# Twelve row buffers, two and four turns between slot stages, and part of the late work behind the slots: an RWKV layer with a routed expert layer

## The chip, the cores and the metric

One core of one Trainium2 chip. The metric is the device time of one execution in microseconds. The profile is of one execution on the same core; its times are counted from the start of its span.

## What is computed

`x` has 16 x 512 = 8192 tokens of 128 float32 features. Two parts are applied one after the other:

```python
x = x + _L0_attn_ref(_layernorm(x), ...)   # RWKV time mix (a scan over 512 steps) and channel mix
x = x + _L0_ffn_ref(_layernorm(x), ...)    # shared expert + one routed expert of 16

logits = hidden @ router_w.T
top_vals, top_idx = jax.lax.top_k(logits, 1)
scores = sigmoid(top_vals) at top_idx, 0 elsewhere
gate, up = split(einsum('nth,nhf->ntf', hidden * scores, gate_up_proj), 2)
expert_sum = einsum('ntf,nfh->nth', up * silu(gate), down_proj).sum(0)
shared = silu(hidden @ shared_gate_w.T) * (hidden @ shared_up_w.T) @ shared_down_w.T
```

Each token goes to a single expert of width 128. The shared expert has width 512 and is applied to all tokens.

## The kernel before, in words

**Rounds.** The tokens are 16 tiles of 512. In 23 rounds (`one_round`, one list per engine) the tiles go through a software pipeline: layer norms, time mix, channel mix, router, and the shared expert. At the end of a tile its rows, the scaled and normed features (128 columns), the token's number (1 column) and the base, that is everything but the routed expert (128 columns), are scattered to a table in DRAM, `sorted_rows`, grouped by expert: four indirect DMAs of GpSimd for each tile. The table is filled up with rows that name no token (`filler`).

**Late halves.** The shared expert is done per half tile of 256 tokens. Twelve halves (`LATE`, line 52) aren't finished before their tile is scattered. Their shares are computed later, kept in SBUF (`sh_of`) and added to `out` at the very end. Three of the twelve (u = 0, 1, 2) are done in the rounds, nine (u = 3 to 11) after them. One of these nine has four steps: step 0 and 1 are a gate and an up product each (`unit_product`, line 394, eight matmul pieces), with the activation on ScalarE (line 695) and the product on VectorE (line 1066); steps 2 and 3 are the two halves of the down product (`unit_down_late`, line 402, eight pieces each), after which ScalarE copies the share out of PSUM (line 698). `late_order` (line 238) lists the 36 steps. The first runs in the rounds, four more ahead of the turns (`STEPS_BEFORE` = 5, line 642), and 31 are spread over the turns by `late_steps` (line 250).

**Slots and turns.** A slot is 128 sorted rows of one expert. There are 80 slots, 40 pairs. The last is always empty: 8192 rows and 16 experts can need at most 79. A pair k goes through these steps:

- SP loads it from `sorted_rows` into a row buffer, two DMAs of 128.5 KB (line 370), after the store of the pair that used the buffer before. There are `RING` = 8 buffers. Ahead of pair 8 (`FILL_PAIR`) SP also issues 16 filler DMAs (line 362).
- TensorE transposes the features of two pairs at a time (line 651), VectorE copies them out of PSUM (line 1075).
- ScalarE copies the two experts' weights (line 814).
- TensorE makes gate and up (lines 658 and 659), ScalarE applies the activation (line 819), VectorE multiplies (line 1083).
- TensorE makes the down product (line 665), VectorE adds it to the base in the row buffer (line 1078).
- GpSimd stores the pair to `out` by token number, two indirect DMAs (line 1215); rows that name no token are left out.

Each engine runs a list of turns m. In turn m come the transposes of pairs m and m+1 (m even), gate and up of pair m - `GU_BEHIND`, the down product, add and store of pair m - `DN_BEHIND`, then the late steps of the turn. `GU_BEHIND` = 1 and `DN_BEHIND` = 2, so there are 42 turns.

**The end.** `add_late` (line 302): SP and ACT wait for the last stores of all row buffers, load six half tiles of `out` each (128 KB), VectorE adds the late shares (line 1093) once all are there, and SP and ACT store them again.

Of the kernel before, what the change touches and what calls it, by code (L numbers as in the profile page):

```python
# [28 lines left out]
P = 128  # L29
# [4 lines left out]
T = S  # L34
# [9 lines left out]
NP = NS // 2  # L44
RING = 8
PACK = 5
# [4 lines left out]
A_TILES, B_TILES, C_TILES = (0, 1, 2, 3, 4, 5, 6, 7, 8, 9, 10, 11, 12, 13, 14), (2, 5, 8, 11, 14), (13, 14, 15)  # L51
LATE = [(0, 1), (1, 1), (3, 1), (4, 1), (6, 1), (7, 1), (9, 1), (10, 1), (12, 1), (13, 1), (15, 1), (15, 0)]
N_LATE = len(LATE)

# [38 lines left out]
def program(nc, x, w_main, w_exp, vecs, out):  # L93
# [4 lines left out]
    with ExitStack() as ctx:  # L98
# [124 lines left out]
        FULL_SLOTS = NTOK // P - NE  # L223
        FILL_PAIR = 8
        FIRST_LATE = len(C_TILES)
        STEPS_BEFORE, LATE_TURN = 5, 1
        GU_BEHIND, DN_BEHIND = 1, 2
        W_BEHIND = GU_BEHIND - 1
# [21 lines left out]
        def late_steps(m):  # L250

            steps = late_order()[STEPS_BEFORE:]
            return [step for i, step in enumerate(steps) if LATE_TURN + i * (NP - 2) // len(steps) == m]

# [14 lines left out]
        def laps(i):  # L269

            return len(range(i, NP, RING))

# [5 lines left out]
        def stored(k):  # L278

            i, lap = k % RING, k // RING + 1  # L280
            if i < 8:
                return f"xout{i}", 32 * lap
            if i == 11:
                return "xout11", 32 * lap
            return f"scat{i - 8}", 16 * G * len(range(i - 8, NT, 3)) + 32 * lap

# [6 lines left out]
        def tl_of(u):  # L293
            return shared[:, u * HALF:(u + 1) * HALF]

        def tl_sem(u):

            if u < 8:
                return f"xr_in{u}", 32 * laps(u)
            return f"x_in{u - 8}", 16 * (NT // XR) + (32 * laps(u) if u < RING else 0)  # L300

        def add_late(eng, units):


            for k in range(NP - RING, NP):
                eng.wait_ge(s[stored(k)[0]], stored(k)[1])
            def place_of(u):
                tile, half = LATE[u]
                row = tile * T + half * HALF
                return out[row:row + HALF, :].rearrange("(p g) d -> p (g d)", g=2)  # L310
            for u in units:
                eng.dma_start(tl_of(u), place_of(u)).then_inc(s[tl_sem(u)[0]], 16)
            for u in units:
                eng.wait_ge(s["tl_add"], u + 1)
                eng.dma_start(place_of(u), tl_of(u)).then_inc(s["tl_out"], 16)
            eng.wait_ge(s["tl_out"], 16 * N_LATE)
# [10 lines left out]
        def _(sp):  # L327
# [30 lines left out]
            for k in range(NP):  # L358
# [10 lines left out]
                for j in range(2):  # L369
                    sp.dma_start(xr[k % RING][:, j, :], sorted_ap[bass.ds(first_rows[at_ + j], P), :]).then_inc(  # L370
                        s[loaded(k)[0]], 16)
            add_late(sp, range(0, N_LATE, 2))


        @block.tensor
        def _(pe):
# [69 lines left out]
            def one_round(n):  # L446
# [8 lines left out]
                for t in at(3):  # L455
                    wait(pe, "xn2T", t)
                    if t == 0:
                        pe.wait_ge(s["w_in1"], 16)
                    wait(pe, "hsg0", t - 2)
                    wait(pe, "sg0", t - 2)  # L460
# [24 lines left out]
                for t in at(3):  # L485
                    wait(pe, "xn2T", t)
                    wait(pe, "hac0", t - 2)
                    wait(pe, "ac0", t - 2)
# [121 lines left out]
                for t in at(3):  # L610
                    wait(pe, "k20", t)
                    wait(pe, "base", t - 2)
                    wait(pe, "hbase", t - 2)
                    wait(pe, "cbase", t - 2)
                    wait(pe, "rv", t - 1)
# [59 lines left out]
        def _(act_e):  # L675
# [147 lines left out]
            for m in range(TURNS):  # L823
                one_turn(m)
            add_late(act_e, range(1, N_LATE, 2))


        @block.vector
        def _(dve):
# [259 lines left out]
            for u in range(N_LATE):  # L1089
                dve.wait_ge(s[tl_sem(u)[0]], tl_sem(u)[1] + 16)  # L1090
                wait(dve, "cbase", NT)
                wait(dve, "lsh", N_LATE)
                v.tensor_tensor(tl_of(u), tl_of(u), sh_of(u), ALU.add).then_inc(s["tl_add"], 1)
# [3 lines left out]
        def _(gp):  # L1097
# [113 lines left out]
            def one_turn(m):  # L1211
                for k in pair(m, DN_BEHIND):
                    wait(gp, "xy", k)
                    for j in range(2):
                        g_.indirect_dma_start(  # L1215
# [43 lines left out]
```

## Time and profile before

| | us |
|---|---|
| median of 3 runs | 559.82 (559.63 to 560.57) |
| profiled execution, its time | 561.58 |
| profiled execution, span from the first to the last instruction | 559.9 |
| mean granted TensorE clock | 0.97 of full |
| busy: TensorE, VectorE, ScalarE, GpSimd | 490.7, 400.1, 322.9, 348.1 |

The busy times are sums over the whole span. The rounds end at about 400 us, and the turns fill the time from there to about 541. A matmul of float32 is recorded in several pieces that overlap, 275 ns each for 128 columns, and its end is modelled.

### The profile page before, as it was taken

Reading aid. Unit: us, or ns where it says so; the run is one execution under the profiler, and the core shown is the slowest. Engines: PE = TensorE matmul, PEld = TensorE weight load, DVE = VectorE, ACT = ScalarE, POOL = GpSimd, SP = SyncE. Lnnn points to the kernel's source line nnn. Section 1 sums busy time; section 2 is a strip of 40 time slices with the busy share of each in tenths; the row PEclk is TensorE's granted clock in tenths of the full one; section 3 lists DMA queues with packets and bytes.
Section 4 is the critical chain, followed back from the end, with each engine's and each line's share of the span. In section 5 each row is a group of like instructions: output and inputs, shape, how many; then the busy total and the mean of one; then the engine's idle time right before and its main releaser. Section 6 shows DMA issues by size and latency. Waiting matters only on the chain.

```text
span 559.9 us, 10321 instructions
## 1 busy us (share of the span) xinstructions
PE 490.7 (88%) x3012; PEld 399.6 (71%) x3012; DVE 400.1 (71%) x1098; ACT 322.9 (58%) x579; POOL 348.1 (62%) x542
## 2 busy tenths in 40 slices
PE   1778999999999999999999999999897879796930
PEld 0336778878778788687777787799796778786830
DVE  3678899998999899997999978745534343333323
ACT  3766977867867678767678664432344353444410
POOL 5364668867887688785878745636245556464660
PEclk9888999999999999999999999999999999898975
DMA  6003201101011011010110000111486344333207
GB/s 207 1 1 145 119 2 58 32 27 55 5 56 58 2 58 38 21 58 2 56 58 10 30 21 20 38 39 39 140 204 172 116 113 119 109 108 93 77 4 226
DMA packets 32424, 38.26 MB, mean 68 GB/s; under 512 B 4946, under 2 KB 28634, under 8 KB 32113
## 3 DMA queue, kind: packets, MB, share of 16 engines
q1 hardware_dynamic: 25008, 23.40, 14.5%
q0 software_dynamic: 5632, 12.63, 6.5%
q10 hardware_dynamic: 1728, 1.57, 0.9%
q8 instruction: 25, 0.41, 0.3%
q14 instruction: 31, 0.25, 0.1%
HBM read 21.15 MB, written 17.47 MB: 69 GB/s over the span
## 4 chain that ended last, share of the span: by engine, by line
PE 60%; DVE 10%; issue 9%; ACT 7%; another core or an unknown queue 6%; POOL 5%; DMA 1%; ACTq 0%; POOLq 0%; SPq 0%; DVEq 0%
PE bank L394 12%; PE bank L387 7%; PE bank L411 5%; PE bank L381 3%; PE bank L402 3%; PE bank L659 3%; PE bank L462 2%; PE bank L479 2%; DVE an L871 2%; PE bank L502 2%; PE bank L658 2%; PE bank L515 2%; PE bank L466 2%; PE bank L490 2%
## 5 line engine op out<-in xcount | busy, mean ns | idle before, releaser
L1215 POOL DMA_INDIRECT out<-shared x80 | 78.8, 985 | 71.3 <-DVE shared L1078 48.8
L394 PE MATMUL bank<-hT,wm 128*128 128x256 f32 x512 | 122.0, 382 | 0.9 <-ACT er L722 0.7
L394 PEld LDWEIGHTS bank<-hT,wm 128*128 128x128 f32 x512 | 94.0, 191 | 18.2 <-issue 7.5
L387 PE MATMUL bank<-wm,k 128*128 128x128 f32 x512 | 63.9, 280 | 2.8 <-ACT k L726 2.8
L387 PEld LDWEIGHTS bank<-wm,k 128*128 128x128 f32 x512 | 62.4, 196 | 4.4 <-ACT k L726 3.6
L1078 DVE TENSOR_TENSOR shared<-bank,shared 128x256 f32<-128x256 f32 x40 | 17.0, 424 | 42.0 <-PE bank L665 22.8
L871 DVE TENSOR_SCALAR an<-a,mvC,smC 128x128 f32<-128x128 f32 x64 | 43.2, 735 | 1.4 <-POOL smC L1125 1.4
L819 ACT ACTIVATE er<-bank 128x256 f32<-128x256 f32 x40 | 15.3, 384 | 48.9 <-remote 22.8
L411 PEld LDWEIGHTS bank<-wm,actA 128*128 128x128 f32 x240 | 30.2, 192 | 6.7 <-issue 6.7
L1204 POOL TENSOR_SCALAR shared<-shared,smA 128x128 f32<-128x128 f32 x64 | 34.6, 549 | 0.3
L411 PE MATMUL bank<-wm,actA 128*128 128x128 f32 x240 | 31.6, 275 | 0.0
L742 ACT ACTIVATE xn1tok<-shared,smA 128x128 f32<-128x128 f32 x64 | 26.2, 479 | 7.1 <-POOL smA L1161 7.1
L1199 POOL TENSOR_TENSOR q<-num,q 128x128 f32<-128x128 f32 x16 | 7.3, 454 | 32.4 <-DVE q L1015 32.4
L1159 POOL TENSOR_TENSOR smA<-smA,half 128x8 f32<-128x8 f32 x16 | 26.4, 1648 | 1.3
L1169 POOL DMA_INDIRECT sorted_rows<-rows,posi x16 | 21.3, 1334 | 9.3 <-DVE posi L934 3.6
L871 DVE TENSOR_SCALAR h<-rows,mvE,smE 128x128 f32<-128x128 f32 x64 | 23.7, 436 | 3.8 <-POOL smE L1125 3.6
L1188 POOL DMA_INDIRECT sorted_rows<-rows,posi x16 | 22.6, 1416 | 4.9 <-issue 4.9
L766 ACT ACTIVATE kr<-bank 128x512 f32<-128x512 f32 x16 | 9.6, 597 | 26.6 <-PE bank L462 26.6
L381 PE MATMUL bank<-ident,xn1tok 128*128 128x128 f32 x64 | 10.1, 283 | 14.6 <-ACT xn1tok L742 14.6
L1141 POOL TENSOR_SCALAR rows<-h,sc 128x128 f32<-128x128 f32 x64 | 22.7, 365 | 0.3
L1174 POOL TENSOR_TENSOR xa<-shared,a 128x512 f32<-128x512 f32 x16 | 21.1, 1316 | 0.5
L930 DVE TENSOR_TENSOR ew<-bank,ew 128x512 f32<-128x512 f32 x16 | 10.9, 683 | 14.6 <-PE bank L515 9.6
(240 smaller groups left out, 1357.6 us busy)
## 6 DMA issues: line engine op xcount, KB each, us to landing
shared<-sorted_rows SPq DMA_DIRECT2D x80, 128.5 KB
shared<-x SPq DMA_DIRECT2D x16, 256.0 KB
wexp<-w_exp SPq DMA_DIRECT2D x2, 1536.0 KB, 8.4
sorted_rows<-filler SPq DMA_DIRECT2D x17, 128.5 KB
out<-shared POOLq DMA_INDIRECT x80
sorted_rows<-rows,posi POOLq DMA_INDIRECT x64
wm<-w_main SPq DMA_DIRECT2D x1, 776.0 KB, 8.1
shared<-out SPq DMA_DIRECT2D x6, 128.0 KB
```

The source lines that it names most:

```text
L381: ins = nc.tensor.transpose(grp(dst, g), grp(src, g), ident[:, :])
L387: ins = mm(grp(acc, g), grp(lhs, g), W(name, f), start=(f == 0 and g == 0), stop=(f == F // P - 1), skip_group_check=True)
L394: ins = mm(dst[:, j * HALF:(j + 1) * HALF], W(name, 2 * pair_ + j), src[:, half * HALF:(half + 1) * HALF], start=True, stop=True)
L411: ins = mm(grp(acc, 2 * half + g), lhs[:, at_:at_ + P], W("down", 2 * pair_ + j), start=(pair_ == 0 and j == 0 and g == 0), stop=(pair_ == ...
L742: ins = af(grp(xn1tok[t % 2], g), grp(xin[t % XR], g), ACT.Identity, bias=smA[t % 3][:, 5, g:g + 1], scale=smA[t % 3][:, 4, g:g + 1])
L871: ins = v.tensor_scalar(grp(dst, g), src(g), mv[:, g, 0:1], rs[:, g:g + 1], ALU.subtract, ALU.mult)
L1141: ins = g_.tensor_scalar(rows[t % 3][:, g, 0:D], grp(h[t % 2], g), sc[t % 2][:, g:g + 1], 1.0, ALU.mult, ALU.mult)
L1159: g_.tensor_tensor(sm[:, 3:5, :], sm[:, 1:3, :], half8[:, :, :], ALU.pow).then_inc(s["pA"], 1)
L1169: g_.indirect_dma_start(sorted_ap, bass.IndirectOffsetOnAxis(posi[t % 3][:, 1:2].bitcast(U32), 0), rows[t % 3][:, 1, :], None).then_inc(s[ ...
L1188: g_.indirect_dma_start(sorted_ap, bass.IndirectOffsetOnAxis(posi[t % 3][:, 0:1].bitcast(U32), 0), rows[t % 3][:, 0, :], None).then_inc(s[ ...
L1204: ins = g_.tensor_scalar(grp(xn0[t % 4], g), grp(xin[t % XR], g), smA[t % 3][:, 0, g:g + 1], smA[t % 3][:, 3, g:g + 1], ALU.add, ALU.mult)
L1215: g_.indirect_dma_start(out, bass.IndirectOffsetOnAxis(xr[k % RING][:, j, D:D + 1].bitcast(U32), 0), xr[k % RING][:, j, D + 1:ROW], None, ...
```

## The change

Seven things are changed:

1. `RING` is 12. Buffers 8 to 11 are the three tiles of rows that the rounds use for the scatter.
2. `GU_BEHIND` is 2 and `DN_BEHIND` 4; the weight copy is one turn later too. There are 44 turns.
3. `STEPS_BEFORE` is 3. The two steps that so remain ((3, 2) and (4, 1)) run in turns 0 and 1, the next 19 spread over turns 4 to 39, and the last 12 in turns 40 to 43, one each in 40, 41 and 42 and nine in 43, behind the turn's own work.
4. The filler DMAs are issued ahead of pair 12.
5. The second slot of the last pair isn't stored, and the waits for that store count 16 less.
6. At the end SP alone waits for the stores and loads the late halves, two halves with one DMA; ACT only stores. VectorE adds half u once its own share is there, not all.
7. The last two late halves change places, and three pairs of waits of TensorE in the rounds change their order.

```diff
-RING = 8
+RING = 12
-LATE = [(0, 1), ..., (13, 1), (15, 1), (15, 0)]
+LATE = [(0, 1), ..., (13, 1), (15, 0), (15, 1)]
...
-        FILL_PAIR = 8
+        FILL_PAIR = 12
-        STEPS_BEFORE, LATE_TURN = 5, 1
-        GU_BEHIND, DN_BEHIND = 1, 2
+        STEPS_BEFORE, LATE_TURN, LATE_AFTER = 3, 4, 12
+        GU_BEHIND, DN_BEHIND = 2, 4
...
             steps = late_order()[STEPS_BEFORE:]
-            return [step for i, step in enumerate(steps) if LATE_TURN + i * (NP - 2) // len(steps) == m]
+            if m < 2:
+                return steps[m:m + 1]
+            if m >= NP:
+                last, at_ = steps[len(steps) - LATE_AFTER:], m - NP
+                return last[at_:at_ + 1] if m < TURNS - 1 else last[at_:]
+            between = steps[2:len(steps) - LATE_AFTER]
+            return [step for i, step in enumerate(between) if LATE_TURN + i * (NP - LATE_TURN) // len(between) == m]
...
-            i, lap = k % RING, k // RING + 1
+            i, lap, none = k % RING, k // RING + 1, 16 if k == NP - 1 else 0
...
+        def stores(k):
+            return range(2) if k < NP - 1 else range(1)
...
-        def add_late(eng, units):
+        def all_stored(eng):
             for k in range(NP - RING, NP):
                 eng.wait_ge(s[stored(k)[0]], stored(k)[1])
...
-            for u in units:
-                eng.dma_start(tl_of(u), place_of(u)).then_inc(s[tl_sem(u)[0]], 16)
+        def load_late(eng):
+            halves_ = out.rearrange("(h p g) d -> p h (g d)", p=P, g=2)
+            for u in range(0, N_LATE, 2):
+                a0, a1 = first_row(u) // HALF, first_row(u + 1) // HALF
+                eng.dma_start(shared[:, u * HALF:(u + 2) * HALF].rearrange("p (h c) -> p h c", h=2),
+                              halves_[:, a0:a1 + 1:a1 - a0, :]).then_inc(s[tl_sem(u)[0]], 16)
...
-            add_late(sp, range(0, N_LATE, 2))
+            all_stored(sp)
+            load_late(sp)
+            store_late(sp, range(0, N_LATE, 2))
...
-            add_late(act_e, range(1, N_LATE, 2))
+            store_late(act_e, range(1, N_LATE, 2))
...
             for u in range(N_LATE):
-                dve.wait_ge(s[tl_sem(u)[0]], tl_sem(u)[1] + 16)
+                if u % 2 == 0:
+                    dve.wait_ge(s[tl_sem(u)[0]], tl_sem(u)[1] + 16)
                 wait(dve, "cbase", NT)
-                wait(dve, "lsh", N_LATE)
+                wait(dve, "lsh", u)
...
-                    for j in range(2):
+                    for j in stores(k):
                         g_.indirect_dma_start(
```

## Rows read from the trace of the kernel before

**Rows 1.** Timeline, 541 to 560 us: start, us, engine, line, operation, count [idle before, releaser]
```profile
541.27 0.42 DVE L1078 TENSOR_TENSOR shared<-bank,shared 128x256 f32<-128x256 f32 x1 [0.80 <-PE bank L665]
...
544.42 0.98 POOL L1215 DMA_INDIRECT out<-shared  x1 [0.30 <-issue]
545.71 0.98 POOL L1215 DMA_INDIRECT out<-shared  x1 [0.30 <-issue]
547.89 2.71 SPq L312 DMA_DIRECT2D shared<-out  x6
...
550.26 1.59 DVE L1093 TENSOR_TENSOR shared<-shared,xn1tok 128x256 f32<-128x256 f32 x4 [8.57 <-DMA shared<-out]
...
554.77 1.43 DVE L1093 TENSOR_TENSOR shared<-shared,ew 128x256 f32<-128x256 f32 x4
```

**Rows 2.** Busy by stretch: us, each engine's busy (count), TensorE clock, DMA share, GB/s
```profile
404.00:541.30 137.30, 112.90 (x811) 105.17 (x809) 52.68 (x115) 58.69 (x144) 74.59 (x76) 0.96 0.43 117
480.00:490.00 10.00, 10.00 (x70) 9.79 (x69) 3.92 (x9) 3.75 (x10) 5.86 (x6) 0.83 0.37 113
490.00:500.00 10.00, 9.56 (x73) 8.94 (x72) 4.39 (x9) 5.29 (x14) 5.60 (x7) 1.00 0.32 94
500.00:510.00 10.00, 5.56 (x38) 5.19 (x37) 2.70 (x6) 2.90 (x7) 4.91 (x6) 0.92 0.48 138
```

**Rows 3.** Waits of 404 to 541.3 us: in total, times, longest
```profile
POOL out L1215 <- DVE shared L1078: 48.8, 15, 14.4
...
ACT er L819 <- remote: 22.8, 8, 4.0
...
DVE shared L1078 <- remote: 16.4, 8, 3.8
...
PE bank L658 <- DVE num L1075: 9.0, 3, 4.4
...
PE bank L665 <- DVE e L1083: 6.7, 8, 2.2
...
PE bank L658 <- ACT th L814: 4.0, 1, 4.0
```

**Rows 4.** Timeline, 452 to 460 us
```profile
452.28 1.10 PE L402 MATMUL bank<-wm,den 128*128 128x128 f32 x8
...
453.22 0.60 PE L651 MATMUL bank<-ident,shared 128*128 128x128 f32 x4
...
455.00 1.89 PE L394 MATMUL bank<-hT,wm 128*128 128x256 f32 x8
...
457.67 0.38 ACT L698 ACTIVATE xn1T<-bank 128x256 f32<-128x256 f32 x1 [5.25 <-remote]
457.73 0.69 DVE L1075 COPY er<-bank 128x512 f32<-128x512 f32 x1 [4.33 <-remote]
...
459.02 0.46 PE L658 MATMUL bank<-er,an 128*128 128x128 f32 x2 [2.13 <-ACT an L814]
```

**Rows 5.** The page's part 4, by engine, over the whole span
```profile
PE 60%; DVE 10%; issue 9%; ACT 7%; another core or an unknown queue 6%; POOL 5%; DMA 1%; ACTq 0%; POOLq 0%; SPq 0%; DVEq 0%
```

**Rows 6.** The chain that ended last, in order of time: start, us, what
```profile
439.35 0.44 PE bank L651 x4
...
440.45 0.22 PE bank L659 x2
440.68 0.45 PE bank L665 x4
441.12 1.73 PE bank L394 x8
...
444.19 0.94 PE bank L402 x8
```

**Rows 7.** Timeline, 400 to 411 us
```profile
402.55 1.89 PE L394 MATMUL bank<-hT,wm 128*128 128x256 f32 x8
```

**Rows 8.** Timeline of SP's queue, 396 to 426 us
```profile
398.74 9.01 SPq L370 DMA_DIRECT2D shared<-sorted_rows  x16
408.96 9.70 SPq L362 DMA_DIRECT2D sorted_rows<-filler  x16
420.09 5.24 SPq L370 DMA_DIRECT2D shared<-sorted_rows  x6
```

**Rows 9.** Line 1215: ns of one min/median/max, first and last start
```profile
L1215 POOL DMA_INDIRECT out<-shared x80: 982/984/1005, 411.0 to 545.7; - x80
```

**Rows 10.** DMA issues of 544 to 560 us: KB, us to landing
```profile
out<-shared SPq DMA_DIRECT2D x6, 128.0 KB, 3.2
```

More of the change, by code:

```diff
@@ L51 @@
 A_TILES, B_TILES, C_TILES = (0, 1, 2, 3, 4, 5, 6, 7, 8, 9, 10, 11, 12, 13, 14), (2, 5, 8, 11, 14), (13, 14, 15)
-LATE = [(0, 1), (1, 1), (3, 1), (4, 1), (6, 1), (7, 1), (9, 1), (10, 1), (12, 1), (13, 1), (15, 1), (15, 0)]
+LATE = [(0, 1), (1, 1), (3, 1), (4, 1), (6, 1), (7, 1), (9, 1), (10, 1), (12, 1), (13, 1), (15, 0), (15, 1)]
 N_LATE = len(LATE)
@@ L278, in stored @@
         def stored(k):
-            i, lap = k % RING, k // RING + 1
+            i, lap, none = k % RING, k // RING + 1, 16 if k == NP - 1 else 0
             if i < 8:
-                return f"xout{i}", 32 * lap
+                return f"xout{i}", 32 * lap - none
             if i == 11:
-                return "xout11", 32 * lap
-            return f"scat{i - 8}", 16 * G * len(range(i - 8, NT, 3)) + 32 * lap
+                return "xout11", 32 * lap - none
+            return f"scat{i - 8}", 16 * G * len(range(i - 8, NT, 3)) + 32 * lap - none
+        def stores(k):
+            return range(2) if k < NP - 1 else range(1)
         def late_act(u):
@@ L296, in tl_sem, with first_row, store_late @@
         def tl_sem(u):
-            if u < 8:
-                return f"xr_in{u}", 32 * laps(u)
-            return f"x_in{u - 8}", 16 * (NT // XR) + (32 * laps(u) if u < RING else 0)
-        def add_late(eng, units):
+            return f"xr_in{u // 2}", 32 * laps(u // 2)
+        def all_stored(eng):
             for k in range(NP - RING, NP):
                 eng.wait_ge(s[stored(k)[0]], stored(k)[1])
[L307 to L310, printed above, removed]
-            for u in units:
-                eng.dma_start(tl_of(u), place_of(u)).then_inc(s[tl_sem(u)[0]], 16)
+        def first_row(u):
+            return LATE[u][0] * T + LATE[u][1] * HALF
+        def load_late(eng):
[4 more added lines that the diff above has]
+                              halves_[:, a0:a1 + 1:a1 - a0, :]).then_inc(s[tl_sem(u)[0]], 16)
+        def store_late(eng, units):
             for u in units:
                 eng.wait_ge(s["tl_add"], u + 1)
-                eng.dma_start(place_of(u), tl_of(u)).then_inc(s["tl_out"], 16)
+                eng.dma_start(out[first_row(u):first_row(u) + HALF, :].rearrange("(p g) d -> p (g d)", g=2), tl_of(u)).then_inc(
+                    s["tl_out"], 16)
             eng.wait_ge(s["tl_out"], 16 * N_LATE)
@@ L458, in one_round @@
                         pe.wait_ge(s["w_in1"], 16)
+                    wait(pe, "sg0", t - 2)
                     wait(pe, "hsg0", t - 2)
-                    wait(pe, "sg0", t - 2)
                     wait(pe, "ew", t + 1)
@@ L486, in one_round @@
                     wait(pe, "xn2T", t)
+                    wait(pe, "ac0", t - 2)
                     wait(pe, "hac0", t - 2)
-                    wait(pe, "ac0", t - 2)
                     wait(pe, "z", t + 1)
@@ L611, in one_round @@
                     wait(pe, "k20", t)
+                    wait(pe, "cbase", t - 2)
+                    wait(pe, "hbase", t - 2)
                     wait(pe, "base", t - 2)
-                    wait(pe, "hbase", t - 2)
-                    wait(pe, "cbase", t - 2)
                     wait(pe, "rv", t - 1)
```

## The prediction

> **What bounds the kernel now.** I read the busy time by stretch first, then the waits of the slot stage, the timeline of one stall, the chain that ended last, and the timeline of the end. The slot stage runs from about 404 us, where TensorE's first transposes of sorted rows follow, to the add of the last pair at 541.27 us [rows 1]. In the 137.3 us of [rows 2] TensorE is busy 112.9, VectorE 52.7, ScalarE 58.7 and GpSimd 74.6 us, and the DMA engines are busy 0.43 of the time: nothing is full, though TensorE is near. TensorE's idle 24.4 us are nearly all waits for copies and products of VectorE and for weight copies of ScalarE [rows 3].
>
> Those waits begin with TensorE's own results reaching their readers late. In [rows 4] the down products of L402 are recorded until 453.38 us, and ScalarE, which waits for them, starts at 457.67; the transposes end by 453.82 and VectorE copies them at 457.73. TensorE meanwhile went on until 456.89 and then stood until 459.02. The profile calls these waits "remote": 22.8 us in 8 waits for the gate's activation, the longest 4.0, and 16.4 us in 8 for the add of the slot's result [rows 3]. Over the whole span such time is 6% of the chain, 34 us [rows 5], about what these waits of the slot stage add up to. Matmul ends are modelled, and no row says what holds the results back; I use only that a reader may have to wait some 4 us more than the matmul takes.
>
> **The work in the slot stage.** A pair of slots costs TensorE, by [rows 6], eight gate and up pieces of 0.11 us (0.89), one down group of 0.45 and half a transpose group of 0.44: 1.56 us, 62.2 for 40 pairs. A late product (eight L394) costs 1.73, a late down (eight L402) 0.94. Before, 31 of the 33 steps that follow the first three lie in the turns, 14 products and 17 downs: 24.2 + 16.0 = 40.2 us. Work is 102.4 of 137.2 us; the other 34.8 are 24.4 idle and 10.4 of slow clock and of ends of groups.
>
> **Fewer late steps in the slots.** After the change 33 steps follow the start of the turns (15 products, 18 downs), 12 of them from turn 40 on. Turns 40 to 42 take one each (product, down, product: 4.4 us) and come before the last down products; turn 43 takes nine, three products and six downs, 5.2 + 5.6 = 10.8 us, behind them. Turns 0 to 39 hold 10 products and 11 downs, 27.6 us. So TensorE has 62.2 + 27.6 + 4.4 = 94.2 us of work to the last slot product instead of 102.4. The first two of these steps used to run before the turns: the second ends 404.4 [rows 7], and the transposes could start instead once the first loads are there. A 128 KB load is used 2.4 us after its issue at the end (547.89 to 550.26, [rows 1]); the fourth load is issued 398.74 + 3 x 0.56 = 400.4 [rows 8], so I put the start at 402.8, 1.3 us earlier.
>
> **More turns between stages.** A turn of TensorE will be (62.2 + 27.6)/40 = 2.25 us. From a transpose to its product there was one turn at the least, from product to down one turn; now there are two of each. Each wait of TensorE thus loses up to 2.25 us: the 3 waits of 9.0 leave 2.3, the 8 of 6.7 (mean 0.84, longest 2.2) leave nothing, the one of 4.0 leaves 1.8: some 4 us. The bounds are 0 and the old 24.4. Of the 10.4 I take half, 5, since clock and group ends go with the gaps: in [rows 2] the clock is 0.83 of 2.4 GHz in 480 to 490 us and 0.92 in 500 to 510, where TensorE is busy only 5.56 of 10 us; it is at 1.0 in 490 to 500, busy 9.56, and a mean in between is time at 1.2 GHz. Beside this row stands the Trainium skill, TensorE: Matmul & The Clock Gate, section HAM oscillation — how this bites in real kernels: a TensorE that waits between short bursts falls to the low clock and pays the slow start again each time. By that rule alone, taking filler work out of the turns would lengthen gaps, and the 10.4 us would stay or grow: 5 us or more on the sum. The row weighs the other way here, since the gaps come from waits that the added turns shorten. The last slot product then ends at 402.8 + 94.2 + 9 = 506.
>
> **GpSimd becomes the pace.** Its stores are issued every 1.29 us when it isn't waiting (544.42, 545.71) and it has 80 of them from 411.0 to 545.7 [rows 1, 9], 103 us of 135; 48.8 us, 14.4 of them ahead of the first, it waits for VectorE's add [rows 3]. Now 79 stores are left. The pipeline fills two turns later, but TensorE starts 1.3 us earlier and early turns are short of down products: work up to the first down is 0.44 + 0.94 + 1.73 + 0.44 + 0.89 + 0.89 + 0.44 + 0.89 + 0.45 = 7.1, so 409.9, with add and issue the first store at about 411.8. The 79th can't start before 411.8 + 78 x 1.288 = 512.3. Held results still starve GpSimd at times before it has a backlog; I add two such waits of 2.9 us (the mean of 22.8 in 8), and put it at 518. The bounds are 512.3, and TensorE's worst case below.
>
> **Twelve buffers.** The 16 fill DMAs now stand behind 24 loads on SP's queue, not 16. SP takes 0.56 us for a load and 0.61 for a fill (9.01 in 16, 9.70 in 16, [rows 8]), so loads 9 to 12 of the pairs are issued by 412.2, not from 420.1, and the fill ends at 422; pair 13 is issued then and is wanted at turn 12, 402.8 + 12 x 2.5 = 433. Nothing waits; if the DMA engines lag, 1 to 2 us. Later a load needs the store twelve pairs back, more slack than eight.
>
> **The tail.** In the execution shown: last store issued 545.71, landed 547.80, twelve 128 KB loads on two queues, first add 550.26, the last group of adds ends 556.2, span end 559.9 [rows 1]. Now SP issues six loads of twice the size in the same 2.7 us, so the bytes land alike; the first add waits for 256 KB, at most some 0.5 us more. ScalarE loses six issues that lay beside SP's. The pairwise waits replace a wait for all late shares. I take the tail as 14.1 us from the last store, give or take 1. The nine steps of turn 43 end at 506 + 10.8 = 517, before the first add at 522.5, so they are hidden; even at the low clock they end at 528, when the last adds run. The reordered waits on TensorE in the rounds and the swap of the last two halves cost nothing: the same conditions are waited for.
>
> **Sum.** 518 + 14.1 = 532.1 us of span, against 559.9. The profiled execution took 561.58 us, 1.7 over its span; the median of the runs is 559.82, 1.8 below that. So span and median agree: **532 us**, range of this case 525 to 541 (GpSimd never starved gives 526.4, two more held stalls of 4 us give 540, and 1 us for the tail).
>
> **Rivals.**
> (B) Depth is eaten: the more TensorE may run ahead, the longer the results stay held, and the 34.8 us of no work remain. Then the last product ends at 402.8 + 94.2 + 34.8 = 531.8, the last store follows 3.2 later (4.5 now, one store less): 535, end 549. For it speaks that TensorE in [rows 4] ran 3.5 us ahead and the results came only then; against it, that the waits of TensorE are mostly under a turn long.
> (C) The clock: with GpSimd pacing, TensorE has small gaps all through and runs a third of its 94 us at 1.2 GHz, 31 us more: product at 537, end 554. The low clock in [rows 2] followed long waits, not small gaps.
> (D) Slower: the late steps ran in time that was waiting anyway, so their leaving shortens nothing, and the last product stays at 540. Then turn 43 follows at the low clock, 21.6 us instead of 10.8, and copy, add, issue and landing (0.4 + 0.4 + 0.3 + 3.2, [rows 10]) end at 566. It decides once the last product is later than 534; at the full clock only from 545. Since a 27 us shift must fail altogether and the clock too, it is small.
> (E) The change doesn't do what it says: the turns are paced one held result each, whatever the depth. Product 540, last store 543, end 557.
>
> **Chances.** A 0.65, B 0.20, C 0.05, D 0.05, E 0.05. The range of 8 in 10 goes from 524.5, just under GpSimd's floor of 526.4, to 550, which takes in B and leaves out C, D, E and what is left at A's edges. A measurement of this kernel can tell 0.2%, 1.1 us: faster by more 0.93, the same 0.02, slower 0.05.
>
> **What would show it.** After: waits called "remote" still there, but TensorE's idle in the slots under 12 us; the gap of GpSimd before its stores well under 20 us apart from the first; 79 stores, the last near 518; late products and downs of turn 43 while stores still run; clock near 1.0. The forecast is wrong if TensorE's idle stays over 20 us (B), if the clock in the slots is under 0.9 (C), or if the adds of the end wait for a late share rather than for the loads (D). The step I trust least is the remaining 9 us.

## The result and the profile after

| | before | after |
|---|---|---|
| median of 20 executions each, us | 560.15 (557.01 to 561.77) | 557.41 (553.35 to 559.85) |
| profiled execution: its time, span | 561.58, 559.9 | 559.75, 558.0 |
| TensorE clock over the span | 0.97 | 0.96 |

The ratio is 0.9949 [0.9932, 0.9966]: faster, but by 0.5% where 5% were forecast. 557.4 us lies above the range of 524.5 to 550.

The busy time by stretch of the kernel after, slot stage: us, then busy time (count) of PE, PEld, DVE, ACT, POOL, then TensorE's clock, DMA share, GB/s.

```profile
404.00:541.00 137.00, 112.38 (x761) 104.79 (x762) 49.87 (x111) 55.35 (x136) 75.70 (x77) 0.89 0.43 120
```

Beside [rows 2] two things are to be seen. TensorE is idle for 24.6 us, as before (24.4): the added turns have shortened nothing in total. And its clock in the slots of this execution is 0.89, not 0.96.

The waits of the slot stage, kernel after: engine, what it waited to write, line, releaser: us in total, times, longest.

```profile
POOL out L1231 <- DVE shared L1093: 41.5, 12, 16.1
ACT er L834 <- remote: 31.7, 10, 6.7
...
DVE shared L1093 <- remote: 13.7, 4, 3.7
DVE rows L1093 <- remote: 13.3, 4, 6.4
...
PE bank L673 <- issue: 8.9, 3, 4.8
DVE er L1090 <- remote: 7.2, 2, 6.5
...
POOL out L1231 <- DVE rows L1093: 4.3, 2, 2.2
```

The waits called "remote" are longer than in [rows 3]: the gate's activation waits up to 6.7 us, not 4.0, and 31.7 in all, not 22.8. Over all readers it is 78.9 us in 25 waits, before 63.6 in 23, the longest 5.2. More depth was met by more delay.

TensorE's own waits changed their kind. Those for ScalarE and VectorE fell from 23.0 us to 11.1, so the added turns did take waits off. But 12.4 us are now waits for nothing that the profile shows ("issue"), where there were 0.5 before, and 2.0 are for a load.

The timeline of one such wait, kernel after: start, us, engine, line, operation, count [idle before, releaser].

```profile
442.02 0.98 POOL L1231 DMA_INDIRECT out<-rows  x1 [2.07 <-DVE rows L1093]
...
445.35 0.60 PE L666 MATMUL bank<-ident,shared 128*128 128x128 f32 x4
...
446.30 0.42 DVE L1093 TENSOR_TENSOR rows<-bank,rows 128x256 f32<-128x256 f32 x1 [2.23 <-remote]
...
446.45 0.39 PE L674 MATMUL bank<-num,rv 128*128 128x128 f32 x2
...
449.16 0.36 PE L680 MATMUL bank<-th,e 128*128 128x128 f32 x1 [0.66 <-issue]
...
449.87 0.27 PE L680 MATMUL bank<-th,e 128*128 128x128 f32 x1 [0.35 <-issue]
...
450.60 0.47 PE L409 MATMUL bank<-hT,wm 128*128 128x256 f32 x1 [0.45 <-issue]
451.03 0.98 POOL L1231 DMA_INDIRECT out<-rows  x1 [0.30 <-issue]
...
453.50 0.69 DVE L1090 COPY er<-bank 128x512 f32<-128x512 f32 x1 [6.45 <-remote]
453.59 0.38 ACT L834 ACTIVATE er<-bank 128x256 f32<-128x256 f32 x1 [6.67 <-remote]
...
454.11 0.41 DVE L1093 TENSOR_TENSOR shared<-bank,shared 128x256 f32<-128x256 f32 x1
```

The transposes are recorded until 445.95 and gate and up (L674) until 446.84. VectorE copies the first at 453.50 and ScalarE reads the second at 453.59, 7.6 and 6.8 us later, within 0.1 us of each other: two engines and two results, let go together. Around them stands what [rows 4] didn't show, since only the engines of the stall were quoted there: GpSimd issues eight stores back to back, from 442.02 to 452.01, and the results come 1.5 us after the last. TensorE is slowed too: from 449.16 its pieces start some 0.7 us apart, with no wait that the profile names. A run of stores stands around the stall of [rows 4] too. The timeline of GpSimd, kernel before:

```profile
449.05 0.98 POOL L1215 DMA_INDIRECT out<-shared  x1 [2.60 <-DVE shared L1078]
...
455.49 0.98 POOL L1215 DMA_INDIRECT out<-shared  x1 [0.30 <-issue]
459.54 0.98 POOL L1215 DMA_INDIRECT out<-shared  x1 [3.06 <-DVE shared L1078]
```

Six stores until 456.47; the held results were read at 457.67 and 457.73. Counting a new run after each gap of over 0.5 us, GpSimd's stores come in 19 runs before (mean 4.2, the longest two 7 and 8) and in 16 after (mean 4.9, four of 8). 17 of the 23 "remote" waits before and 16 of the 25 after end 0.8 to 1.6 us behind the end of a run. The others end during one, such as the add at 446.30 above: a run doesn't hold everything until its end.

The rest of the profile, beside the forecast's own steps: 79 stores, from 413.69 to 543.21 (forecast 411.8 and 518); the last slot product ends at 539.63 (506). The end of the kernel after:

```profile
539.02 0.61 PE L680 MATMUL bank<-rv,e 128*128 128x128 f32 x4
...
542.00 0.42 DVE L1093 TENSOR_TENSOR shared<-bank,shared 128x256 f32<-128x256 f32 x1 [1.43 <-remote]
...
543.21 0.98 POOL L1231 DMA_INDIRECT out<-shared  x1 [1.15 <-DVE shared L1093]
544.17 0.60 ACT L710 ACTIVATE ev<-bank 128x512 f32<-128x512 f32 x1 [5.22 <-remote]
...
545.45 3.14 SPq L321 DMA_DIRECT2D shared<-out  x6
...
549.58 0.69 DVE L1081 TENSOR_TENSOR actB<-sgB,bank 128x512 f32<-128x512 f32 x1 [1.97 <-PE bank L409]
550.18 1.43 DVE L1109 TENSOR_TENSOR shared<-shared,xn1tok 128x256 f32<-128x256 f32 x4
...
550.98 2.12 PE L417 MATMUL bank<-wm,actB 128*128 128x128 f32 x16 [0.56 <-ACT ew L713]
```

The late steps of turn 43 now stand in the tail, and the first add of a late share comes 6.97 us after the last store (4.55 in [rows 1]), straight behind the multiplication of a late step (L1081). The tail is 14.8 us from the last store, 0.7 more than forecast.

### The profile page after: what moved, and what is told of

It is laid out like the page before. It is cut to its first block, busy times and chain, and to the rows that moved or that the text cites. A ratio compares the mean times of both kernels' runs of the same rounds, so it can differ in the third digit from the quotient of the medians.

```text
span 558.0 us, 10310 instructions
## 1 busy us (share of the span) xinstructions
PE 499.3 (89%) x3012; PEld 406.6 (73%) x3012; DVE 397.8 (71%) x1098; ACT 322.8 (58%) x579; POOL 346.4 (62%) x541
## 4 chain that ended last, share of the span: by engine, by line
PE 58%; DVE 11%; issue 10%; POOL 7%; ACT 6%; another core or an unknown queue 5%; DMA 1%; ACTq 0%; SPq 0%; DVEq 0%; POOLq 0%
PE bank L409 12%; PE bank L402 6%; PE bank L426 5%; PE bank L673 3%; PE bank L674 3%; DVE an L886 3%; PE bank L396 3%; PE bank L417 3%; PE bank L680 2%; PE bank L477 2%; PE bank L494 2%; PE bank L517 2%; PE bank L530 2%; PE bank L481 2%
## 5 line engine op out<-in xcount | busy, mean ns | idle before, releaser
L409 PE MATMUL bank<-hT,wm 128*128 128x256 f32 x512 | 125.6, 389 | 4.8 <-issue 2.3
L409 PEld LDWEIGHTS bank<-hT,wm 128*128 128x128 f32 x512 | 95.3, 194 | 24.6 <-issue 11.8
L1231 POOL DMA_INDIRECT out<-shared x55 | 54.1, 983 | 55.2 <-DVE shared L1093 40.0
L834 ACT ACTIVATE er<-bank 128x256 f32<-128x256 f32 x40 | 15.3, 381 | 54.4 <-remote 31.7
L1093 DVE TENSOR_TENSOR shared<-bank,shared 128x256 f32<-128x256 f32 x28 | 11.8, 422 | 35.9 <-PE bank L680 17.1
L1231 POOL DMA_INDIRECT out<-rows x24 | 23.6, 983 | 13.7 <-issue 6.7
L886 DVE TENSOR_SCALAR h<-rows,mvE,smE 128x128 f32<-128x128 f32 x64 | 22.8, 420 | 3.6 <-POOL smE L1141 3.5
L781 ACT ACTIVATE kr<-bank 128x512 f32<-128x512 f32 x16 | 9.6, 597 | 26.6 <-PE bank L477 26.6
```

The costliest lines, as they stand in the source:

```text
L409: ins = mm(dst[:, j * HALF:(j + 1) * HALF], W(name, 2 * pair_ + j), src[:, half * HALF:(half + 1) * HALF], start=True, stop=True)
L886: ins = v.tensor_scalar(grp(dst, g), src(g), mv[:, g, 0:1], rs[:, g:g + 1], ALU.subtract, ALU.mult)
L1231: g_.indirect_dma_start(out, bass.IndirectOffsetOnAxis(xr[k % RING][:, j, D:D + 1].bitcast(U32), 0), xr[k % RING][:, j, D + 1:ROW], None, ...
```

## What holds the results: experiments on the stores

The theory after the first comparison: while GpSimd issues stores back to back, what TensorE has finished isn't told to its readers. Rivals: the loads or the traffic as a whole do it, or TensorE's own density of work. All ratios below are to the kernel before on the same chip. Each run's edit is to the kernel after, unless said otherwise. The chips differ (see below), so it matters that every run without a "remote" wait shares its chip with runs that have them: x_no_store and x_sp_store with x_no_load and x_no_late; x_gp_plain and b_no_store with p_2x128 and b_2x128; p_1x512 with p_2x512. x_no_store, x_sp_store, x_no_late, x_gp_plain and b_no_store have only two executions each.

**x_no_store.** `out` is filled with zeros early, loads wait for the add twelve pairs back.

```diff
-                    for j in stores(k):
-                        g_.indirect_dma_start(out, ..., xr[k % RING][:, j, D + 1:ROW], ...)
```

> The changed kernel without the stores of the slots: GpSimd stores nothing in the turns, a load waits for the add of the pair twelve back instead of its store, and out is filled with zeros early in the rounds so that the late halves can be loaded. Left out: the routed rows never reach out. In the changed kernel the last slot product ends at 539.6 us, and waits called remote add up to 79 us between 404 and 541. Theory 'stores' (TensorE's results are held back while GpSimd's indirect stores run): the remote waits go to under 8 us and the last slot product ends by 515; span about 525. Rival 'loads' or 'dense TensorE' (the hold belongs to loads into the row buffers, or to TensorE's own stream of short matmuls): remote waits stay at 60 us or more, the last slot product at 530 to 541, span 545 to 556.

520.94 us, 0.9324 [0.9232, 0.9415]. No wait on "remote" is left. Busy time by stretch, and the last slot product in TensorE's timeline:

```profile
404.00:541.00 137.00, 106.17 (x823) 101.75 (x822) 57.70 (x128) 60.05 (x144) 0.00 (x0) 0.99 0.40 113
404.00:500.00 96.00, 93.72 (x744) 90.35 (x744) 50.59 (x111) 56.50 (x137) 0.00 (x0) 1.00 0.48 128
```

```profile
500.80 0.61 PE L682 MATMUL bank<-rv,e 128*128 128x128 f32 x4
```

To 500 us TensorE is idle for 2.3 us of 96, at the full clock, and the last slot product ends at 501.4. That is the TensorE of the forecast (506), and better. Without the stores the forecast's sum for TensorE holds.

**x_sp_store.** SP stores the rows with plain DMAs in slot order, eight pairs behind the loads; the routed order is left out.

```diff
+                if k >= 8:
+                    store_direct(k - 8)
```

> The changed kernel with the slots stored by SP with plain DMAs of the same size instead of by GpSimd's indirect ones (the rows go to out in slot order, not to their tokens, which is left out). Theory 'stores by GpSimd': remote waits under 8 us, last slot product by 515, as without stores. Theory 'writes to memory' (any store of this traffic does it): remote waits stay above 60 us and the last slot product at 530 to 541. Theory 'dense TensorE' or 'loads': like the changed kernel too, so that this run alone doesn't tell those from writes.

535.28 us, 0.958 [0.9487, 0.9673]. Again no "remote" wait, though the same bytes are stored. What TensorE waits for is now loads, in one wait of 10.2 us above all; that load stands on SP's queue behind the 16 filler DMAs and a store. Waits of TensorE:

```profile
PE bank L678 <- DMA shared<-sorted_rows: 11.9, 5, 10.2
```

So it isn't the bytes of the stores that hold results.

**x_no_load.** Only the first twelve pairs are loaded; later pairs use the rows again, and VectorE's add waits for the buffer's store in place of the load.

```diff
-                for j in range(2):
+                for j in range(2 if k < RING else 0):
```

> The changed kernel with loads for the first twelve pairs alone; later pairs use the rows that lie in their buffer. Left out: the rows of pairs 12 to 39. Theory 'stores': remote waits stay above 60 us, last slot product at 530 to 541. Theory 'loads': they go to under 8 us after about 415 us and the last slot product ends by 515, as GpSimd then paces. Theory 'dense TensorE': no change.

555.34 us, 0.9911 [0.9879, 0.9944]. The "remote" waits stay. Waits of the slot stage:

```profile
ACT er L835 <- remote: 24.0, 8, 6.7
...
DVE shared L1096 <- remote: 13.1, 4, 5.7
DVE rows L1096 <- remote: 10.1, 2, 5.1
```

So the loads aren't the cause: without them the gate's activation waits up to 6.7 us, as with them, and another wait (`ACT ev`) is 8.0 us.

**x_no_late.** The late steps from the turns on are left out.

```diff
-            steps = late_order()[STEPS_BEFORE:]
+            return []
```

> The changed kernel without the 33 late steps in and behind the turns (left out: the shares of late halves 3 to 11). TensorE's work up to the last slot product falls from 94 to 62 us. Theories 'stores' and 'loads' (a held result paces each turn whatever TensorE has to do): the last slot product stays within 10 us of 539.6, the remote waits at 60 us or more. Theory 'dense TensorE': the remote waits shrink in proportion to the work, by a third or more, and the last slot product ends by 520. If the forecast's view held (work plus a few short waits), GpSimd would pace: last store at 513 to 518.

551.91 us, 0.9878 [0.9733, 1.0023]. Busy time by stretch, and a wait:

```profile
404.00:541.00 137.00, 83.12 (x560) 78.75 (x558) 42.81 (x101) 47.61 (x120) 77.75 (x79) 0.82 0.43 120
```

```profile
ACT er L834 <- remote: 30.2, 10, 6.7
```

TensorE is busy for 29 us less in the slots, its last slot product ends 9 us earlier (530.7), and the kernel isn't clearly faster: the stage isn't paced by TensorE's work. Most of the work taken away turns into idle time and a lower clock (0.82). And the holds are as long as ever, so TensorE's density doesn't make them.

**x_gp_plain.** GpSimd issues the stores as before, but as plain DMAs in slot order.

```diff
-                        g_.indirect_dma_start(out, ...)
+                        g_.dma_start(to, xr[k % RING][:, j, D + 1:ROW])
```

> The changed kernel with GpSimd storing the slots by plain DMAs in slot order (left out: the rows' way to their tokens), everything else as it is. If any DMA that GpSimd issues back to back holds TensorE's results: remote waits of 50 us or more, time 550 to 562. If it is the indirect addressing: no remote waits, and the time between the 521 without stores and the 535 with SP's stores, or up to 545 if GpSimd's issue paces.

523.78 us, 0.9358 [0.933, 0.9386], and no "remote" wait. The timeline of GpSimd:

```profile
442.56 1.07 POOL L1234 DMA_DIRECT2D out<-rows  x2 [2.44 <-DVE rows L1094]
443.90 1.07 POOL L1234 DMA_DIRECT2D out<-rows  x2 [0.27 <-DVE rows L1094]
446.62 1.07 POOL L1234 DMA_DIRECT2D out<-shared  x2 [1.65 <-DVE shared L1094]
```

A plain DMA takes GpSimd 0.54 us against 0.98 and 0.30 of issue for an indirect one, so it drains a pair in 1.1 us and its runs stay short, up to four stores. Four plain ones last 2.4 us; four indirect ones last 4.8, and on the same chip they went with waits of up to 3.8 us (b_2x128). Whether the indirect form matters or only the length of the runs, this run can't say.

**b_no_store.** The kernel before without its stores, in the same way as x_no_store.

> The kernel before, with one and two turns of depth, eight buffers and the late steps in the slots, without the slots' stores (left out: the routed rows never reach out). The changed kernel without stores took 520.9 us. Theory of the forecast, depth takes waits off TensorE: here waits of TensorE of 10 us or more remain, and with 12 us of late work more in the slots the time is 535 to 545. Theory 'without held results depth has nothing to do': TensorE is busy nearly throughout, and the time is 521 to 533, by the late work alone.

527.53 us, 0.9425 [0.9393, 0.9456]. All waits of TensorE in the slot stage:

```profile
PE bank L660 <- ACT an L816: 1.0, 1, 1.0
PE bank L667 <- DVE e L1085: 0.8, 1, 0.8
```

One and two turns are enough when nothing is held: 1.8 us of waits. The depth that the change adds mends waits that only the held results cause. The two kernels without stores, 527.5 and 520.9 us on two chips, are 0.9425 and 0.9324 of the kernel before: without holds the whole change may be worth some 1%, but the two intervals overlap.

## The parts of the change

**d_depth_back.** `GU_BEHIND`, `DN_BEHIND` as before, all else of the change.

```diff
-        GU_BEHIND, DN_BEHIND = 2, 4
+        GU_BEHIND, DN_BEHIND = 1, 2
```

> The changed kernel with one and two turns between the stages as before; twelve buffers, late steps behind the slots (twelve, from turn 40 on), and the new end are kept. Theory 'GpSimd's run sets the hold, and depth only makes runs longer': within 3 us of the changed kernel's 557.4. Theory of the forecast (each added turn takes 2.25 us off each wait of TensorE): 10 us or more slower than the changed kernel, 567 or more.

561.53 us, 0.9995 [0.9973, 1.0017], between the two theories and nearer to the first; the longest "remote" wait is 5.4 us, and they add up to 71.2. TensorE's waits for ScalarE and VectorE are 26.7 us, against 11.1 with the depth. The depth is worth about 0.5%, all that the change gains.

**d_late_inside.** All late steps in turns 4 to 39.

```diff
-            between = steps[2:len(steps) - LATE_AFTER]
+            between = steps[2:]
```

> The changed kernel with all late steps between turns 4 and 39, none behind the slots. Theory 'GpSimd's run': TensorE's work in the slots isn't what paces, so the last slot product moves by less than 4 us, and the time stays within 4 us of 557.4. Theory of the forecast (TensorE's work counts in full): 12 us of late work come back into the slots, and the time is 565 or more.

556.87 us, 0.9906 [0.988, 0.9932]. TensorE's work in the slots is back, and the stage is no longer for it. Busy time by stretch:

```profile
404.00:541.00 137.00, 114.02 (x816) 106.28 (x814) 51.60 (x115) 56.80 (x142) 76.02 (x78) 0.96 0.41 117
```

The clock is back at 0.96 too, and the last slot product ends at 535.4, 4.2 us earlier (under 4 was expected). The late steps behind the slots bring nothing, and cost some 0.4%: the interval of this kernel ends at 0.9932, where that of the changed one begins.

**d_ring8.** `RING` and `FILL_PAIR` of 8.

```diff
-RING = 12
+RING = 8
```

> The changed kernel with eight row buffers and the fill ahead of pair 8, as before. Theory of the forecast for this part: loads 9 to 12 come some 8 us later, which hardly matters, but with four turns of depth and a load that needs the store eight pairs back, a run of eight stores (four pairs) and a landing leave TensorE short: 2 to 8 us slower than the changed kernel, 560 to 566. Theory 'GpSimd's run' alone: eight buffers cut GpSimd's runs and change nothing beyond 2 us.

566.89 us, 1.0134 [1.009, 1.0178]. Waits of TensorE:

```profile
PE bank L666 <- DMA shared<-sorted_rows: 29.1, 16, 5.2
```

Deeper turns keep a buffer longer, and with eight buffers TensorE waits 29.1 us for loads; the time lies just above the 560 to 566 of the forecast's theory. The twelve buffers are what makes the depth possible: some 1.9% between the two kernels. Its GpSimd runs are cut to at most five stores, mostly two or four, and the "remote" waits fall to 21.8 us, the longest 3.7, though nothing was done to the stores. The time is lost all the same: shorter holds alone don't make the kernel faster.

## Breaks in GpSimd's runs

If results are held in runs of stores, a break in a run should let them through. GpSimd adds a small tile that it then waits for, after every n-th pair:

```diff
+                    if k % 2 == 2 - 1 and k < NP - 2:
+                        const(g_.tensor_tensor(kr[0][:, 0:128], kr[1][:, 0:128], kr[2][:, 0:128], ALU.add))
```

**p_2x512 and p_1x512**: 512 columns, after every second pair and after every pair.

> The changed kernel with a pause of GpSimd after every second pair of stores: an addition of 128x512 that nothing uses and that GpSimd waits for (such an addition took 1.32 us in the rounds). Reading behind it: in both traces TensorE's results go through for about 4 us after a run of back-to-back stores begins, are then held, and come free about 1 us after the run's last store. Theory 'run': a break of over 1 us after every four stores (5.2 us) leaves holds of 1 to 2 us at most; remote waits fall from 79 us to under 25, and though GpSimd does 26 us of work more, the last store isn't later than the changed kernel's 543.2; time 545 to 556. Rival 'number of stores' (each store holds TensorE for a fixed share, breaks or not): remote waits stay at 60 us or more and the pauses add to the time: 565 to 580.

565.92 us, 1.0058 [1.0036, 1.0079]. No run is longer than four stores, the longest "remote" wait is 3.9 us, and they add up to 31.8, not 79. So the rival's count of stores fails; but the time is far above the 545 to 556 of theory 'run', since a break costs GpSimd some 1.8 us (by the rows of p_1x512 below, 0.99 + 1.29 + 0.79 instead of 1.29) and the last store is issued only at 550.91.

> The same pause after every pair, so that a run is two stores, 2.6 us. Theory 'run': no held results at all (remote waits under 8 us), and GpSimd paces at 2.58 + 1.6 = 4.2 us a pair: slots last 40 x 4.2 = 168 us, time 580 to 595. Rival 'number of stores': remote waits stay at 60 us or more, time above 600.

600.17 us, 1.0658 [1.0626, 1.0689], above the expected 595: the pace is 4.36 us a pair, far too slow. But with runs of two stores no "remote" wait is left at all, with the same 79 stores. They also come at a slower rate, and TensorE waits 36 us for loads, so this run alone doesn't part the length of a run from the rate. The timeline of GpSimd, p_1x512:

```profile
443.83 0.99 POOL L1231 DMA_INDIRECT out<-shared  x1 [0.79 <-POOL kr L1236]
445.12 0.97 POOL L1231 DMA_INDIRECT out<-shared  x1 [0.30 <-DVE shared L1093]
446.11 1.29 POOL L1236 TENSOR_TENSOR kr<-kr 128x512 f32<-128x512 f32 x1
```

**p_3x128, q_2x128, q_3x128**: 128 columns; after every third pair; with the late steps inside the turns after every second; and after every third.

> The changed kernel with a shorter pause of GpSimd (an addition of 128x128, some 0.4 us, and the 0.8 us that its wait took in the run before) after every third pair. Theory 'run': a run of six stores is 7.6 us, the hold ends 1 us after it, and GpSimd goes on from its backlog after 1.2 us where it stood 2 to 3 us before. Holds stay near 3 us each, which the four turns of depth cover; GpSimd's stores span 79 x 1.29 + 13 x 1.2 = 117 us instead of 131, and the time is 543 to 552. Rival: the gap after a run can't be shortened, since TensorE needs 2 us and more from the release to the next add, and GpSimd has no backlog then: 555 to 562.

553.56 us, 0.9879 [0.985, 0.9909], between the two expected ranges. The holds did not get short: the "remote" waits add up to 74.4 us, the longest 6.0. What this kernel gains by its break isn't explained by shorter holds, and stays open.

> The changed kernel with all late steps in the slots and the short pause after every second pair. Theory 'run': runs of four stores, holds of 1 to 2 us; stores span 79 x 1.29 + 20 x 1.2 = 126 us, time 547 to 555. Rival (GpSimd has no backlog): 555 to 562.

554.45 us, 0.9895 [0.9869, 0.9922], as expected, though the "remote" waits, 55.6 us in 31, reach 3.9 us and not 2.

> The changed kernel with all late steps in the slots and the short pause after every third pair. Theory 'run': as with the late steps behind, 543 to 552; TensorE's 106 us of work in the slots leave less room. Rival (GpSimd has no backlog): 555 to 562.

558.58 us, 0.9962 [0.9941, 0.9983], in the rival's range. The shorter break pays with the late steps behind the slots. It doesn't add to the gain of the late steps inside the turns (0.9906): after every second pair it changes nothing clear of noise, after every third the kernel is slower.

**p_2x128**: the change and a short break after every second pair.

> The changed kernel as it is (late steps behind the slots) with the short pause after every second pair. Theory 'run': as q_2x128, ratio to before 0.9895, or a little less as TensorE has 12 us less to do in the slots: 0.983 to 0.991. If the late steps behind the slots delay the adds of the end: 0.990 to 0.995.

552.99 us, 0.9875 [0.9853, 0.9897]: the lowest ratio of the complete kernels, with p_3x128. Waits of the slot stage, GpSimd's timeline, and the last slot product:

```profile
POOL out L1231 <- DVE shared L1093: 19.1, 4, 14.7
...
DVE shared L1093 <- remote: 9.8, 4, 3.7
```

```profile
436.02 0.97 POOL L1231 DMA_INDIRECT out<-shared  x1 [0.30 <-issue]
437.30 0.97 POOL L1231 DMA_INDIRECT out<-shared  x1 [0.30 <-issue]
438.27 0.49 POOL L1236 TENSOR_TENSOR kr<-kr 128x128 f32<-128x128 f32 x1
439.55 0.99 POOL L1231 DMA_INDIRECT out<-rows  x1 [0.80 <-issue]
```

```profile
518.24 0.61 PE L680 MATMUL bank<-rv,e 128*128 128x128 f32 x4
...
536.31 0.97 POOL L1231 DMA_INDIRECT out<-shared  x1 [0.31 <-issue]
```

From one store's start to the next it is 1.28 us, and 2.25 with the break between, so a break costs 1 us, 19 of them some 18. GpSimd's waits for VectorE's adds in `shared`, without the first, fall from 25.4 us in 11 to 4.4 in 3. The "remote" waits add up to 33.0 us, the longest 3.7. TensorE's last slot product ends at 518.9 instead of 539.6, and from 404 to 518 us its clock is 0.99. GpSimd now sets the time by its own issue: 413.63 for the first store, 78 x 1.28, 19 x 0.97 for the breaks and 4.4 of waits give 536.3, where the last store is.

**b_2x128**: the kernel before with that break alone.

> The kernel before with the same short pause after every second pair and nothing else changed. Theory 'depth gives GpSimd the backlog that makes a pause cheap': here GpSimd waits for adds anyway and its runs are already four to six stores, so a pause gains little or costs: ratio 0.995 to 1.01. Theory 'the hold alone matters': 0.985 to 0.992, as with depth.

553.71 us, 0.9895 [0.987, 0.9919]. The expectation of little gain was wrong: the break pays about as much without the change as with it (0.9875 beside it on the same chip, the intervals overlap).

## Two runs on a chip that holds nothing

**x_gp_plain5** was to tell the indirect form from the length of the runs: plain stores, and three small DMAs more a pair, so that runs are as long.

> As the run with plain stores by GpSimd, but with three small plain DMAs more for each pair (a constant tile, 128 x 16, to memory that nothing reads), so that GpSimd issues 5 DMAs of 0.54 us a pair and stands in back-to-back runs as long as with the indirect stores. Left out as there: the rows' way to their tokens. If long runs of any DMAs of GpSimd hold TensorE's results: remote waits of 30 us or more, time 545 to 560. If it is the indirect form: no remote waits, and GpSimd's issue paces at 2.7 us a pair or less: 522 to 535.

**p_2x16** was to find the shortest break that pays.

> The changed kernel with the shortest pause after every second pair: an addition of 128x16, with its wait about 0.9 to 1.0 us between the stores. If 1 us is too short to free the held results (they came about 1 us after the last store of a run, and gaps of 0.7 us freed nothing): long holds are back in some runs and the ratio is 0.99 or more. If it is enough: 0.984 to 0.988, a little better than with 1.3 us (0.9875).

Both ran on a chip on which the kernel before took 537.53 us, not 560. There x_gp_plain5 took 538.82 us, 1.0035 [0.9999, 1.0071], and p_2x16 546.3 us, 1.0186 [1.0141, 1.0231]. Neither trace has a "remote" wait in the slots, p_2x16 with indirect stores in runs of four, which on another chip went with waits of up to 3.7 us (p_2x128). No trace of the kernel before was taken on this chip. If it too holds nothing there, as its time suggests, a break has nothing to mend, and x_gp_plain5, which holds nothing where indirect stores hold nothing either, tells nothing. Why the chips differ stays open, and so does whether the indirect form or the length of the run matters. The changed kernel itself wasn't run there, so how much of the 1.9% is the break and how much the change is open too.

## Why the prediction was wrong

**The premise.** "Each wait of TensorE thus loses up to 2.25 us" failed as a saving of time. It takes the delay of a result as given, some 4 us, and lets depth absorb it. The waits for copies and products, put at "some 4 us", did fall, from 23.0 to 11.1, but 12.4 us of waits without a named releaser came instead. The runs show a delay that goes with GpSimd's runs of stores and mostly ends about 1 us behind them (x_no_store: none without stores; p_1x512: none with runs of two). Depth lets more adds gather, so that GpSimd's runs are longer (mean 4.9 stores, not 4.2; four of eight, not one), and the longest hold is 6.7 us, not 5.2. That depth lengthens the holds through the runs is argued from one trace of each kernel and of d_depth_back, not shown. It is rival B's mechanism, at about rival E's time, and that the numbers of E fit is luck, since E has one held result a turn: product 540, last store 543, end 557 were its numbers, and 539.6, 543.2 and 558.0 were measured. The chain of cause, GpSimd needs adds, adds need held products, the hold ends when GpSimd has run dry, is read from the timelines. That GpSimd's indirect stores are its condition is shown by the experiments; that the length of a run matters is supported (p_1x512, p_2x512, d_ring8) and p_3x128 doesn't fit it well; what in the chip couples them isn't shown.

**The remaining 9 us.** From TensorE's start of turns to the last product, 402.6 to 539.6 are 137.0 us. With 94.2 of work, 42.8 are left, not 9, and 8.0 more than the 34.8 of before. TensorE is busy for 111.4 us of this stretch, so idle time is 25.6 of the 42.8, where I had put 4, and 17.2 are clock and ends of groups, where I had put 5. So the 8.2 us of late work that left the slots were given back almost whole, most of it by the clock. The clock of 0.89 settles what the forecast weighed, and against the forecast. The Trainium skill, TensorE: Matmul & The Clock Gate, section HAM oscillation — how this bites in real kernels, has a waiting TensorE fall back to the low clock between bursts. By that rule the 10.4 us stay or grow, and the trace agrees: they grew to 17.2, and with all late work away the clock fell to 0.82. Fewer late steps alone don't lower it: p_2x128 has the same steps in the slots and shorter holds, and its clock there is 0.99 until 518 us.

**GpSimd becomes the pace.** It did, but the term for its starving was too small: "I add two such waits of 2.9 us". From the gaps and the first store it comes out as measured. 413.69 + 78 x 1.288 = 514.15. The waits for adds are 25.4 us in 11 (`shared`), 4.3 in 2 (`rows`) and the last one of 1.15; less the 0.30 us that each shares with an ordinary gap, they add 26.6. Three longer gaps without a named releaser add 2.4, and the sum is 543.2. So these waits are 14 of 2.2 us, not two of 2.9. Before, the same excess over 1.288 us a store was 32.9 us, now it is 29.1. These 3.8 us and the store left out (1.3), less a first store 2.7 us later and a tail 0.6 longer, are the 1.9 us between the two spans.

**Start and tail.** The first store came 1.9 us later than forecast and 2.7 later than before [rows 9], since TensorE, which did start at 402.59 as forecast (402.8), then waited 2.04 us for the second pair's load. SP issued its first load at 399.71, 1.0 us later than in [rows 8]. The tail is 14.8, not 14.1. The late steps weren't hidden: "end at 506 + 10.8 = 517, before the first add at 522.5". The first add stands at 550.18, and TensorE's last late steps end at 553.1, one of their activations held for 5.22 us. Adds that wait for a late share were the sign of D. The first add does stand straight behind a late step's multiplication; how long its load alone would have kept it isn't shown.

**What was right.** The saved 80th store; twelve buffers, which the depth needs (d_ring8); the remark that the late steps ran in waiting time (rival D: taking them out shortens nothing, as d_late_inside shows); and TensorE's own time without holds, 501.4 against the 506 of the forecast. The 9 us were named as the step trusted least. The reading stopped one step short: [rows 4] showed two results released together and [rows 3] called it "remote", and GpSimd's timeline over the same 8 us wasn't laid beside them.

## What to carry to other kernels

When readers of TensorE's results wait with a releaser that the profile calls remote, lay the timelines of all engines over the stall before you price more buffering: look for what starts and ends with it, here runs of indirect stores of GpSimd. Where the delay comes from such runs, depth alone buys little (0.5% here), and a short wait after every fourth store took 1.0% off the kernel before (b_2x128); other breaks cost more than they gave (p_2x512, p_1x512). Work taken off an engine that isn't the pace came back here as idle time and a lower clock, as long as the holds stayed. And such a coupling may be absent on another chip, where the changed kernel with a break was 1.9% slower than the kernel before.

## What the runs showed of the hardware

- On the chips where the kernel before takes 559 to 563 us, VectorE and ScalarE waited up to 5.2 us (before), 6.7 (after) and 8.0 (x_no_load) for results of TensorE while GpSimd issued indirect stores back to back. In the two stalls quoted the results came 1.2 us (before) and 1.5 us (after) behind the run; over the slot stage 17 of 23 and 16 of 25 such waits ended 0.8 to 1.6 us behind one. TensorE itself started pieces only some 0.7 us apart late in the longest run. Without its stores the kernel before is 5.7% faster (b_no_store), which takes in the holds, GpSimd's own pace, and an end that waits for no store.
- Stores by SP's queue (x_sp_store) or plain ones of GpSimd (x_gp_plain) held nothing, each on a chip where indirect ones did.
- One chip ran the kernel before in 537.5 us. Two kernels traced there (p_2x16, x_gp_plain5) held nothing.
- GpSimd is taken for 0.98 us by an indirect store of 128 rows (after) and 0.54 us by a plain one (x_gp_plain).
